# Expert rows by indirect gather in a fused Mamba and mixture-of-experts layer, slot lists by one-hot products on TensorE

## What is computed

```python
# attn: a Mamba block, E = 512 channels, N = 16 states
rn = xn * rsqrt(mean(xn * xn) + EPS) * norm_w
x = silu(conv_b + causal_conv4(rn @ in_w.T, conv_w))
delta = softplus(x @ wd1.T @ wd2.T + wd2_b); B = x @ wB.T; C = x @ wC.T
h = exp(delta * A) * h + (delta * x) * B          # step by step over 1024 tokens
y = (sum over n of h * C) + x * W_D               # x * W_D is "the D term"
attn = xn + (y * silu(rn @ skip_w.T)) @ out_w.T   # silu(...) is "the gate"
# ffn: 8 experts of 512 columns, each token goes to the 2 with the LOWEST gates
gates = softmax(xn @ Wr); inds = top_k(-gates, 2); scores = picked / sum
ffn = sum over the 2 picks of score * ((silu(xn @ W1[e]) * (xn @ V1[e])) @ W2[e])
```

## Time and profile before

| | us |
|---|---|
| median of 3 runs | 1393.11 (1392.39 to 1397.13) |
| the profiled execution, its own time | 1397.35 |
| its span, first to last instruction | 1395.5 |
| DVE busy | 1168.4 (84%) |
| PE busy | 1096.8 (79%) |
| ACT busy | 1077.9 (77%) |
| POOL busy | 1051.2 (75%) |
| mean granted TensorE clock | 0.892 of full |

### The profile page before, as it was taken

One profiled execution on the slowest core, in us unless ns is written; L12 is line 12 of the kernel. 1 busy time (PEld: TensorE's weight loads), 2 busy tenths in 40 slices (PEclk: granted clock), 3 DMA queues, 4 the chain that ended last, 5 costly groups with the idle time before them and its releaser, 6 DMA issues.

```text
span 1395.5 us, 20412 instructions
## 1 busy us (share of the span) xinstructions
PE 1096.8 (79%) x5172; PEld 779.7 (56%) x5172; DVE 1168.4 (84%) x2155; ACT 1077.9 (77%) x2263; POOL 1051.2 (75%) x921
## 2 busy tenths in 40 slices
PE   4378356466589888989989888989899898888865
PEld 2267344344356656666666666666566666565644
DVE  6665759867688898999989889999989889998995
ACT  3787356768589797979889897979798897978763
POOL 0475357888778887979788887879798787878775
PEclk9656566667699999999999999999999999999987
DMA  6595294443945454454545454443545454444535
GB/s 211 163 289 175 75 324 142 146 152 116 257 124 147 135 137 129 119 146 132 154 123 147 134 147 136 131 136 112 159 125 154 134 144 130 143 122 111 140 121 170
DMA packets 111377, 209.08 MB, mean 150 GB/s; under 512 B 21328, under 2 KB 71632, under 8 KB 111184
## 3 DMA queue, kind: packets, MB, share of 16 engines
q1 hardware_dynamic: 93456, 185.88, 41.2%
q0 software_dynamic: 17520, 21.83, 9.2%
q10 hardware_dynamic: 288, 0.07, 0.0%
HBM read 171.43 MB, written 40.25 MB: 152 GB/s over the span
## 4 chain that ended last, share of the span: by engine, by line
PE 43%; POOL 19%; issue 13%; ACT 12%; DMA 7%; DVE 5%; POOLq 0%; DVEq 0%; ACTq 0%
POOL part L782 12%; PE yps L872 9%; PE bankH L979 6%; PE bankV L1001 5%; DMA acc<-mst 5%; PE bankG L897 5%; PE bankX L1009 4%; POOL xbuf L821 4%; ACT aexp L558 3%; DVE hb L1117 2%; PE bankG L907 2%; PE bankV L941 2%; POOL acc L833 2%; PE bankG L909 2%; PE bankX L952 1%
## 5 line engine op out<-in xcount | busy, mean ns | idle before, releaser
L782 POOL TENSOR_TENSOR part<-hb,bcr 128x512 f32<-128x512 f32 x512 | 691.4, 1397 | 211.3 <-DVE hb L1117 117.1
L1117 DVE TENSOR_TENSOR_SCAN hb<-aexp,carry,bps 128x256 f32<-128x256 f32 x768 | 550.5, 736 | 65.9 <-ACT aexp L558 44.2
L872 PE MATMUL yps<-idn,part 128*128 128x128 f32 x2048 | 346.1, 302 | 189.2 <-POOL part L782 173.1
L558 ACT ACTIVATE aexp<-delta,Am 128x256 f32<-128x256 f32 x1024 | 447.1, 502 | 29.4 <-DVE hb L1117 20.4
L872 PEld LDWEIGHTS yps<-idn,part 128*128 128x128 f32 x2048 | 258.6, 154 | 308.6 <-POOL part L782 236.0
L1096 DVE TENSOR_TENSOR bps<-ups,bcr 128x512 f32<-128x512 f32 x512 | 346.5, 677 | 15.4 <-DMA bcr<-brows 7.2
L1117 DVE TENSOR_TENSOR_SCAN hb<-aexp,bps 128x256 f32<-128x256 f32 x256 | 169.0, 677 | 45.9 <-ACT aexp L558 44.7
L979 PE MATMUL bankH<-w,scr 128*128 x288 | 140.1, 609 | 15.8 <-ACT mst L675 11.6
L1001 PE MATMUL bankV<-v,scr 128*128 x288 | 136.8, 597 | 0.3 <-ACT xin L607 0.3
L1009 PE MATMUL bankX<-w,scr 128*128 x576 | 136.2, 379 | 0.0
L833 POOL DMA_INDIRECT acc<-scr,idx x72 | 115.0, 1598 | 25.5 <-issue 8.2
(11 more groups left out here) (160 smaller groups left out, 1629.3 us busy)
## 6 DMA issues: line engine op xcount, KB each, us to landing
bcr<-brows SPq DMA_DIRECT2D x256, 512.0 KB, 3.9
xbuf<-scr SPq DMA_DIRECT2D x8, 1161.0 KB, 8.6
scr<-xbuf SPq DMA_DIRECT2D x72, 128.0 KB, 3.8
w<-in_W SPq DMA_DIRECT2D x2, 4096.0 KB, 23.4
xch<-in_x SPq DMA_DIRECT2D x16, 256.0 KB, 4.2
w<-in_x SPq DMA_DIRECT2D x4, 1024.0 KB, 9.8
acc<-scr SPq DMA_DIRECT2D x16, 256.0 KB, 2.3
v<-in_V SPq DMA_DIRECT2D x1, 4096.0 KB, 14.0
```

Of the source, the lines that this page charges most:

```text
L558: nc.scalar.activation(aexp[:, w % EXP_SLOTS, i, :], delta[:, c % 2, e, :], ACT.Exp, scale=Am[:, e, n:n + 1]).then_inc(s_a, 1)
L782: nc.gpsimd.tensor_tensor(part[:, w % PART_SLOTS, :, :], hb[:, w % STATE_SLOTS, :, :], bcr[:, w % (2 * ROW_PAIRS), CH:2 * CH].unsqueeze(1) ...
L872: mm = pe.matmul(yps[:, s, i * P:(i + 1) * P], part[:, w % PART_SLOTS, i, s * P:(s + 1) * P], idn[:, :], start=(n == 0 and s == 0 and i == ...
L1117: v.tensor_tensor_scan(hb[:, w % STATE_SLOTS, i, :], aexp[:, w % EXP_SLOTS, i, :], bps[w % 2][:, i, :], first, ALU.mult, ALU.add).then_inc ...
```

## The change

The scatter of token copies goes. In its place:

- **The rows.** Piece R also stores the normalised tile to a DRAM buffer `xt` (SP), and ACT waits for the store of two pieces before when it writes into that place again. The zero fills of `xbuf` (8 DMAs of 1161 KB) go; one of 128 KB stays.
- **The slot list.** The router turns slots into a tile and a lane within it (8 small DVE operations for 2 casts). In chunk 1, eight rounds M of 8 columns each: DVE makes two one-hot tables (576 and 1024 elements wide), POOL multiplies the first by token number and by score (two operations of 576), PE adds up 8 products of 128 x 144 in bank X. Piece MF reads the bank: `meta` (scores) and `idx` (token numbers).
- **The gather.** POOL fetches tile j with one indirect DMA from `xt` (`gather`), two tiles ahead, where SP's `load_tile` did it.
- **Experts from chunk 2 on:** 4 tiles in chunk 2, 5 in chunks 3, 4, 5 and 14, 6 in chunks 6 to 13. The router's tables move beside W2, so V1 and W1 are loaded at the end of the R pieces, and W2 after MF.
- **The D term on TensorE.** Four more products (a diagonal matrix `dg` of W_D, x2) into the bank of O1. O2 comes before O1 and uses banks G and V. DVE multiplies the bank by the gate (two operations of 512 columns); POOL's gate is gone.
- **One Silu.** The convolution is written into `x2` at once, and X2 is one Silu of 1024 columns where there were two of 512, each in a place of its own.
- All tables of places are new.

```diff
+    0: [0, 2, 5, 6, 6, 8, 8, 10, 11, 13, 13, 15, 18, 21, 22, 22, 28, 28],
...
+    "other": [3, 6, 7, 7, 12, 12, 12, 14, 14, 17, 17, 18, 22, 24, 24, 24, 27, 27],
...
-DISPATCH = {1: 10, 2: 6}
...
-O_PIECES = [("O1",), ("O2", 0), ("O2", 1), ("O3", 0), ("O3", 1)]
+FFN_TILES = {c: {2: 4, 3: 5, 4: 5, 5: 5, 14: 5}.get(c, 6) for c in range(2, 15)}
+ROUNDS, ROUND = 8, TOPK * TT // 8
+O_PIECES = [("O2", 0), ("O2", 1), ("O1",), ("O3", 0), ("O3", 1)]
...
-    "other": [2, 3, 3, 15, 17],
...
+    "other": [1, 1, 3, 14, 19],
...
-    "other": [0, 0, 5, 7, 10, 11, 12, 13, 16, 16, 18, 23, 25, 26, 28, 29, 29, 30],
...
+    "six": [0, 0, 4, 7, 8, 9, 11, 14, 14, 17, 17, 20, 26, 27, 28, 29, 29, 30],
...
     if c == 0:
         work = [("R", i) for i in range(TT // 2 + 2)]
-    elif c in DISPATCH:
-        first = sum(DISPATCH[k] for k in DISPATCH if k < c)
-        work = [("D", first + i) for i in range(DISPATCH[c])]
-        if first + DISPATCH[c] == TT // 2:
-            work.append(("FB", -1))
+    elif c == 1:
+        work = [("M", r) for r in range(ROUNDS)] + [("MF",), ("FB", -1)]
...
-    "POOL": {"FC": 3, "O3": 5, "CW": 1, "O2": 3, "RES": 5, "D": 1, "CV": 5, "O1": 3, "U": 5, "R": 2},
...
+    "POOL": {"FC": 2, "O3": 6, "CW": 1, "CV": 2, "MF": 1, "D": 5, "O2": 1, "DL": 2, "FA": 2, "RES": 6, "O1": 1, "R": 1},
...
-            def load_tile(j):
-                if j >= 2:
-                    wait_full(sp, "X", ("FB", j - 3))
-                sp.dma_start(tok[:, j % 2, :], xbuf[j * P:(j + 1) * P, 0:D]).then_inc(ld_xs[j % 2], 16)
...
+                    if i == 0:
+                        sp.wait_ge(zero_set, 1)
+                        sp.dma_start(xt[TOKENS:TOKENS + P, :], empty).then_inc(xt_zero, 16)
+                    sp.wait_ge(xn_r, 2 * (i + 1))
+                    sp.dma_start(xt[2 * i * P:2 * (i + 1) * P, :].rearrange("(s p) d -> p s d", p=P),
+                                 tok[:, 2 * i % 4:2 * i % 4 + 2, :]).then_inc(xt_out[i % 2], 16)
...
+                elif kind == "R" and piece[1] == TT // 2:
...
+                    sp.dma_start(v1[:, :].rearrange("p (e k f) -> p e k f", e=EXPERTS, k=KD), V1.rearrange("e (k p) f -> p e k f", p=P)).then_inc(ld_v1, 16)
...
+                elif kind == "MF":
+
...
+                    sp.dma_start(w2[:, :].rearrange("p (e k f) -> p e k f", e=EXPERTS, k=FF // P), W2.rearrange("e (k p) f -> p e k f", p=P)).then_inc(ld_w2, 16)
...
+                    c = piece[2]
+                    act.wait_ge(conv, KE * (c + 1))
+                    nc.scalar.activation(x2[:, c % 2, :, :], x2[:, c % 2, :, :], ACT.Silu).then_inc(x2r, 1)
...
+                            act.wait_ge(xt_out[i % 2], 16 * (i // 2))
...
+            def gather(j):
+
+                if j >= 2:
+                    wait_full(pool, "X", ("FB", j - 3))
+                nc.gpsimd.indirect_dma_start(out=tok[:, j % 2, :], out_offset=None, in_=xt,
+                                             in_offset=bass.IndirectOffsetOnAxis(ap=idx[:, j:j + 1], axis=0)).then_inc(ld_xs[j % 2], 16)
...
-                elif kind == "D":
-                    if piece[1] == 0:
...
-                    for t in (2 * piece[1], 2 * piece[1] + 1):
-                        pool.wait_ge(xn_r, TT + t + 1)
-                        for k, sl in enumerate((sl1, sl2)):
-                            nc.gpsimd.indirect_dma_start(
-                                out=xbuf, out_offset=bass.IndirectOffsetOnAxis(ap=sl[:, t:t + 1], axis=0),
-                                in_=ring[t % RING][:, k, :], in_offset=None).then_inc(disp[t % RING], 16)
+                elif kind == "M":
...
+                    nc.gpsimd.tensor_tensor(whose, which, back[:, at].unsqueeze(2).to_broadcast([P, ROUND, JT]), ALU.mult).then_inc(val_set, 1)
+                    pool.wait_ge(val_set, 3 * r + 2)
+                    nc.gpsimd.tensor_tensor(which, which, score[:, at].unsqueeze(2).to_broadcast([P, ROUND, JT]), ALU.mult).then_inc(val_set, 1)
+                elif kind == "FB" and piece[1] == -1:
+                    pool.wait_ge(idx_set, 2)
+                    wait_rows(pool)
+                    gather(0)
+                    gather(1)
+                elif kind == "FA" and piece[1] + 2 < JT:
+                    gather(piece[1] + 2)
...
+                    pe.wait_ge(dg_set, KE)
                     pe.wait_ge(y_taken, 2 * (c + 1))
                     for q, b in enumerate("HV"):
...
+                        for i in range(2):
+                            pe.matmul(bank[b][:, i * CH:(i + 1) * CH], dg[:, 2 * q + i, :], x2[:, c % 2, 2 * q + i, :],
+                                      start=(i == 0), stop=False, skip_group_check=True)
                         for s in range(SUB):
                             for i in range(2):
                                 e = 2 * q + i
-                                mm = pe.transpose(bank[b][:, i * CH + s * P:i * CH + (s + 1) * P],
-                                                  yT[:, s, e * P:(e + 1) * P], idn[:, :])
+                                mm = pe.matmul(bank[b][:, i * CH + s * P:i * CH + (s + 1) * P], yT[:, s, e * P:(e + 1) * P], idn[:, :],
...
+                elif kind == "M":
+                    r = piece[1]
+                    pe.wait_ge(hot_set, r + 1)
+                    pe.wait_ge(val_set, 3 * r + 3)
+                    for k in range(ROUND):
+                        mm = pe.matmul(bank["X"][:, 0:2 * JT], hot[r % 2][:, k, :], vals[r % 2][:, k, :],
+                                       start=(r == 0 and k == 0), stop=(r == ROUNDS - 1 and k == ROUND - 1))
+                    mm.then_inc(placed if r < ROUNDS - 1 else full["X"], 1)
...
+                link(v.tensor_copy(whole[:, :], ratio))
+                link(v.tensor_copy(ratio, whole[:, :]))
...
+                link(v.tensor_tensor(tile, ratio, under0, ALU.subtract))
+                link(v.scalar_tensor_tensor(out=lane, in0=under0, scalar=float(P), in1=rest, op0=ALU.mult, op1=ALU.add))
...
+                if r >= 2:
+                    dve.wait_ge(placed, r - 1)
+                at = slice(r * ROUND, (r + 1) * ROUND)
...
+                v.tensor_tensor(vals[r % 2][:, :, JT:2 * JT], tiles, tile[:, at].unsqueeze(2).to_broadcast([P, ROUND, JT]), ALU.is_equal).then_inc(val_set, 1)
+                if r == 0:
+                    dve.wait_ge(ones_set, 2)
+                v.tensor_tensor(hot[r % 2], steps.unsqueeze(1).to_broadcast([P, ROUND, P]),
+                                lane[:, at].unsqueeze(2).to_broadcast([P, ROUND, P]), ALU.is_equal).then_inc(hot_set, 1)
...
                     for q, b in enumerate("HV"):
+                        wait_taken(dve, "GV"[q], ("O2", q, c))
                         wait_full(dve, b, piece)
-                        for i in range(2):
-                            e = 2 * q + i
-                            ins = v.scalar_tensor_tensor(out=y1[:, e, :], in0=x2[:, c % 2, e, :], scalar=WD[:, e:e + 1],
-                                                         in1=bank[b][:, i * CH:(i + 1) * CH], op0=ALU.mult, op1=ALU.add)
-                        ins.then_inc(free[b], 1)
-                        if c == CHUNKS - 1 and c in DVE_GATE:
-                            apply_gate(dve, v, q, c)
-                elif kind == "O2" and piece[2] < CHUNKS - 1 and piece[2] in DVE_GATE:
-                    apply_gate(dve, v, piece[1], piece[2])
+                        v.tensor_tensor(y1[:, 2 * q:2 * q + 2, :], bank[b][:, :].rearrange("p (k t) -> p k t", k=2), tqO[:, q, :, :],
+                                        ALU.mult).then_inc(free[b], 1)
...
+                elif kind == "MF":
+                    wait_full(dve, "X", piece)
+                    v.tensor_copy(meta[:, :], bank["X"][:, JT:2 * JT]).then_inc(idx_set, 1)
+                    where = rt[:, 0].rearrange("p t e -> p (t e)")[:, 0:JT]
+                    v.tensor_scalar(where, bank["X"][:, 0:JT], idb[:, TT:TT + 1], 0.25, ALU.add, ALU.add).then_inc(free["X"], 1)
+                    wait_taken(dve, "X", piece)
+                    v.tensor_copy(idx[:, :], where).then_inc(idx_set, 1)
```

245 lines of the change are left out of this document (111 added, 134 removed), and 15 rows, old and new, of tables (B_PLACES, F_PLACES, LATER).

## The result

The changed kernel took 1353.28 us (median of 4 runs, 1352.63 to 1355.61) where the kernel before, run beside it, took 1395.12 (1392.39 to 1399.15): a ratio of 0.9707 with a 95% interval of 0.9677 to 0.9736. The forecast was 1353. It was right to the microsecond by luck. Most of its stages were off by 5 to 17 us, with both signs. What follows is mostly about these errors.

A forecast was written before the change was run, and what follows sets the result against it. DVE was taken as the bound in chunks 3 to 13, POOL's scatter bursts held up chunks 1 and 2, ACT held chunk 0. Stage terms summed to -40.2 from 1397.35, giving 1357.1, less 4.24: 1353; range 1331 to 1378.

The forecast's parts named there:

- the 104.4: Chunk 1: DVE busy 97.8 us plus idle 5.6 plus 1 for reading the bank, so +2.4 against 102.0.
- the 6 us for the exclusion between DVE and GpSimd: Chunk 1, rounds M: 0.4 us extra for each of 16 DVE table operations with two SBUF inputs; bounds 0 and 20.
- The stall of 6 for W2's load: Chunk 2: stall 4 us for W2, landing near 18.4 against 14.4 of rows in hand, plus 2 for starting expert work.
- The Silu term (-2.6): Chunk 0: one Silu instead of two saves ACT a table switch and the switch back, 2 x 1.28 us.
- The wait of ACT for stores, taken at +1: Chunk 0: ACT must wait for the store of the tile pair before last, +1 us.
- the +1.9 of the forecast: Chunk 0: the router gets 8 operations and a scan more and loses two casts, about +1.9 us.
- -0.4 for D term and gate: Chunks 6 to 13: DVE's busy time falls by 0.4 us a chunk.
- -1.0 for Silu and bank G: Chunks 6 to 13: ACT loses two switches and the wait before the second gate; half of 1.94 us goes, -1.0 a chunk.
- +0.2 for the gathers: Chunks 6 to 13: PE stands 1 to 2 us twice a chunk for gathered rows; DVE sees 0.1 of each, +0.2.
- still covered, but its slack falls from 13 to 7.5: Chunks 6 to 13: POOL's busy time goes from 64.45 to 69.8 us a chunk with the gathers, still covered.
- Rival B: POOL sets the chunk at 1.6 us a gather: six-tile chunks 79, five-tile 76.3, kernel 1380; chance 0.11.
- The sum: Whole kernel: stage changes, mostly DVE busy time plus idle time per chunk, total -40.2 us against the profiled 1397.35.

## Why the prediction was right, and where it was not

**Chunks 1 and 2: the dispatch held them.** The gain came, and more than forecast; that it is the scatters' is argued from rows, since no run put them back. The change moved the 4 MB loads as well, and before it DVE had stood 6.98 in chunk 1, which the prediction lays to them, and 5.4 in chunk 2 for a row load. It also moved the order: with the old later places, and no scatter, chunk 1 took 122.8 and chunk 2, with its four tiles, 85.8. Without the scatters chunk 1 runs at 94.50 with DVE busy for 90.59: idle 3.9, not 6.6. DVE was to be busy for 97.8, and the 104.4 failed at one term above all, the 6 us for the exclusion between DVE and GpSimd. The rounds' operations in chunk 1 (busy us, mean ns):

```profile
L1228 DVE TENSOR_TENSOR w<-w 128x1024 f32<-128x1024 f32 x8 | 9.7, 1218 | 0.0
L1225 DVE TENSOR_TENSOR w<-w 128x576 f32<-128x576 f32 x8 | 6.8, 847 | 0.0
L799 POOL TENSOR_TENSOR w<-w 128x576 f32<-128x576 f32 x8 | 16.5, 2065 | 13.5 <-DVE w L1225 13.5
L801 POOL TENSOR_TENSOR w<-w 128x576 f32<-128x576 f32 x8 | 9.2, 1149 | 0.6
```

DVE's tables took 16.5 where 15.6 was counted without the lock: it cost DVE 0.9, not 6. GpSimd paid. L799 and L801 are operations of one shape, and L799 took 2.07 against 1.15; it starts while DVE's long table runs. The timelines of GpSimd and of DVE:

```profile
165.94 2.07 POOL L799 TENSOR_TENSOR w<-w 128x576 f32<-128x576 f32 x1 [1.26 <-DVE w L1225]
```

```profile
165.78 1.22 DVE L1228 TENSOR_TENSOR w<-w 128x1024 f32<-128x1024 f32 x1
```

The prediction had the case of the earlier trace rows, where one step on DVE took 3.18 beside GpSimd and three had taken 1.53, and made it the rule for all 16 tables. The convolution steps also got cheaper: twelve at 626 ns, 7.5 us, where the same twelve of chunk 1 had taken 9.5 before, the one of 3.18 among them. No run took the rounds apart; this part rests on rows alone.

**Chunk 2.** 76.7 against 82.7. The stall of 6 for W2's load did not come: its 17.0 us passed beside the row loads, DVE shows no wait for them in the chunk but for one of 0.9 whose releaser is not known, and it was busy for 68.75, not 71.1.

**Chunk 0.** The Silu term (-2.6) was too small by at least a fifth, the fills were counted at nothing and cost 3 us or more, and the table of places was not costed at all, though it moved nearly every piece. The wait of ACT for stores, taken at +1, doesn't appear among its waits in the chunk. The router part came out near the +1.9 of the forecast: from its first DVE operation at 132.9 to the end of the chunk it took 24.6 us where the kernel before took 22.0.

**Chunks 6 to 13: the step that failed.** By its own steps the prediction had -0.4 for D term and gate, -1.0 for Silu and bank G, +0.2 for the gathers. Measured one part at a time: the D term -0.9 (634.9 against 627.7), the Silu -1.3, the gathers +2.35. The first two were too small and the last too small by a factor of twelve: "still covered, but its slack falls from 13 to 7.5". The slack was there (10 us a chunk) and did not cover them. The three measured parts make +0.2 a chunk and the chunks grew by 0.9, so that some 6 of the 7.1 us are in none of them; the old order of pieces in the kernel before is one candidate, and no run shows it. The price of a gather itself was good, 1.02 against the 1.3 assumed, and the 4.1 us to landing, longer than the 3.2 of the earlier trace rows, did no harm. The forecast looked for the damage at the transposes that wait for rows, 3.1 us over the eight chunks, and it was at the transposes of `part`, whose waits are 28.8 us with gathers and 20.2 without. They were 28.0 before the change.

**Rival B** (GpSimd sets the chunk, 79 with six tiles and 76.3 with five) was therefore nearer in chunks 3 to 13, at 78.5 and 77.8, though it had asked for 1.6 us a gather to get there, and the forecast total held because chunks 0 to 2 gave 30 us more than they were given. That a five-tile chunk is hardly faster than a six-tile one says the same: neither was held by the busy time of an engine. The sum took DVE's busy time plus a fixed idle time for the length of a chunk, and that was the common error. Chunk 14 (+1.2 where -3.5 was forecast) was not taken apart.

**Chunk 15.** 6.6 us came where 0.5 was expected. GpSimd's last gates are gone and DVE's wait before the last additions is 2.1 instead of 5.8; no run separates them.

**Readings that were off and did no harm.** The prediction put 40 scatters into chunk 1 and 24 into chunk 2; the trace has 35 and 30. GpSimd was then to be busy for 55 and about 66 us there, and it was for 69.4 and 57.2, still not the bound. The eight operations of the earlier trace rows that take 1.89 are four calls in the kernel, so the D term's four products cost 2.05 us a chunk and not 0.9; most of it filled the stand at L867. And without PE's wait for gathers the sum gives 1351, not 1350.

## What to carry to other kernels

An engine that feeds an in-order chain has no usable slack just because it idles: price work that is added to it by what stands behind it in its queue, and measure the slope with work that nobody waits for. Before taking work off an engine, look at what its next piece waits for; products in front of a wait cost nothing here, and taking them away made the kernel 19 us slower. And a sum over stages that comes out right proves none of its terms: compare stage by stage, where here errors of -14, -10, -6, +9 and +17 us nearly cancelled.

## What the runs showed of the hardware that was not expected

An indirect gather of 128 rows of 1 KB holds GpSimd for 1.02 us, as long as the scatters did (0.995), and lands 4.1 us after its issue.

Where operations of DVE and GpSimd with both inputs in SBUF met, either could be the one that took longer: one step on DVE 3.18 where three took 1.53, and GpSimd's product 2.07 instead of 1.15 now. The section "Who interferes with whom" of the Trainium skill's page "SBUF — State Buffer" says that the order of issue decides which of the two is blocked. GpSimd's product agrees: it starts 0.16 after DVE's table and ends 1.01 after it. The step on DVE does not by its recorded start, 203.91, which is 0.40 ahead of the first of the two `part` operations behind which it ended.

TensorE left gaps of 1.7 to 1.8 us at the higher level and its clock fell behind some of them and not behind others of the same length: eight products took 3.33 us where they take 1.89, and the chunks with such a spell were 1.3 to 1.5 us longer. In chunk 0 a filler that raised the granted clock from 0.69 to 0.86 brought no time, and what the clock alone is worth there is open.
